# Second attention of a hybrid block: eight pairs of batches instead of four groups of four, and the causal mask of the row maxima added by VectorE head by head instead of by mask products on TensorE

## The reference, cut to what matters

```python
def _L2_attn_ref(x, wq, wk, wv, wo, ...):          # x: 16 batches, 256 tokens, 32 channels
    q = _rope(proj(wq, ...).reshape(B, S, 4, 8), cos, sin).transpose(0, 2, 1, 3)
    k = _rope(proj(wk, ...).reshape(B, S, 4, 8), cos, sin).transpose(0, 2, 1, 3)
    v = proj(wv, ...).reshape(B, S, 4, 8).transpose(0, 2, 1, 3)
    scores = jnp.einsum('bhqd,bhkd->bhqk', q, k) * 8 ** -0.5
    causal = jnp.triu(jnp.ones((S, S), dtype=bool), k=1)
    scores = jnp.where(causal[None, None], -jnp.inf, scores)
    attn = jax.nn.softmax(scores, axis=-1)
    out = jnp.einsum('bhqk,bhkd->bhqd', attn, v)
    return out.transpose(0, 2, 1, 3).reshape(B, S, 32) @ wo.T
```

## Time and profile before

| | |
|---|---|
| median of 3 runs | 640.49 us (640.01 to 640.94) |
| the profiled execution | 640.55 us, of which the span from the first to the last instruction is 638.7 us |
| busy over the whole span | TensorE 456.9 us (72%), VectorE 239.4 us (37%), ScalarE 273.0 us (43%) |
| the second attention's stretch 201.76 to 291.77 us of the span | from its first mask product to the first product of the next layer norm |

### The profile page before, as it was taken

The page is one execution under the profiler, slowest core; times in us unless marked ns, Lnnn a source line. Parts: engine busy times, 40 slices in busy tenths (PEclk is TensorE's granted clock), DMA queues, the critical chain, the costliest instruction groups (busy, mean ns, idle before and its releaser), DMA issues.

```text
span 638.7 us, 10438 instructions
## 1 busy us (share of the span) xinstructions
PE 456.9 (72%) x4078; PEld 221.0 (35%) x4082; DVE 239.4 (37%) x576; ACT 273.0 (43%) x822; POOL 21.7 (3%) x21
## 2 busy tenths in 40 slices
PE   5466666667888698876466666665677999799544
PEld 3222222223443344442233333333224553455211
DVE  1422222224644456632500000000086894587443
ACT  2333333334565255553333333333465554755411
POOL 1000000000002500000000000000030000000000
PEclk9655555556899899997655555555579998999966
DMA  5000000000000000000000000000041100000001
GB/s 209 0 2 1 0 1 2 1 0 2 1 2 1 1 1 2 2 2 0 1 1 0 1 1 1 1 0 1 0 90 38 42 9 1 2 2 2 2 9 35
DMA packets 8377, 7.43 MB, mean 12 GB/s; under 512 B 3202, under 2 KB 8066, under 8 KB 8196
## 3 DMA queue, kind: packets, MB, share of 16 engines
q1 hardware_dynamic: 8324, 6.70, 3.5%
HBM read 4.99 MB, written 0.52 MB: 9 GB/s over the span
## 4 chain that ended last, share of the span: by engine, by line
PE 64%; ACT 17%; DVE 9%; issue 7%; DMA 1%; SPq 1%; DVEq 1%; ACTq 0%
PE ps L410 18%; ACT arena L431 11%; PE ps L368 4%; PE ps L377 4%; PE ps L817 3%; PE ps L1122 3%; PE ps L1085 2%; PE ps L386 2%; PE ps L1101 2%; PE ps L811 2%; PE ps L326 2%; PE ps L1089 2%; DVE arena L1720 2%; PE ps L1143 1%; PE ps L1274 1%
## 5 line engine op out<-in xcount | busy, mean ns | idle before, releaser
L410 PE MATMUL ps<-arena,wsb 16*16 16x16 f32 (+1 forms) x1024 | 131.2, 206 | 103.8 <-ACT arena L431 102.9
L431 ACT ACTIVATE arena<-ps 16x16 f32<-16x16 f32 (+1 forms) x512 | 96.0, 188 | 183.5 <-PE ps L410 183.5
L410 PEld LDWEIGHTS ps<-arena,wsb 16*16 16x16 f32 (+1 forms) x1024 | 76.5, 118 | 192.4 <-ACT arena L431 184.5
L440 DVE TENSOR_TENSOR X<-X,ps 128x128 f32<-128x128 f32 x8 | 2.3, 288 | 137.4 <-PE ps L377 137.4
L1503 ACT ACTIVATE arena<-ps 128x512 f32<-128x512 f32 x72 | 40.8, 595 | 26.8 <-PE ps L1089 24.3
L1906 DVE TENSOR_TENSOR arena<-arena,ps 128x512 f32<-128x512 f32 x64 | 42.0, 682 | 17.3 <-ACT arena L1503 13.5
L1720 DVE TENSOR_REDUCE arena<-ps 128x4 f32<-128x512 f32 x48 | 30.6, 684 | 29.6 <-PE ps L817 29.6
L1374 ACT ACTIVATE arena<-ps 128x512 f32<-128x512 f32 x48 | 25.6, 593 | 25.4 <-PE ps L833 25.4
L817 PE MATMUL ps<-arena 32*128 32x512 f32 x96 | 25.5, 677 | 4.3 <-ACT arena L1374 3.3
L1085 PE MATMUL ps<-csb 128*128 128x512 bf16 x64 | 24.7, 385 | 2.7 <-DVE sq L464 1.8
L823 PE MATMUL ps<-arena 32*128 32x512 f32 x96 | 25.5, 679 | 1.2 <-ACT arena L1374 1.2
(11 more groups left out here) (300 smaller groups left out, 680.7 us busy)
## 6 DMA issues: line engine op xcount, KB each, us to landing
wsb<-weights SPq DMA_DIRECT2D x1, 2056.5 KB, 9.8
arena<-w SPq DMA_DIRECT2D x20, 64.0 KB
arena<-xn SPq DMA_DIRECT2D x9, 128.0 KB, 2.6
wsb<-weights SPq DMA_DIRECT2D x1, 549.5 KB, 4.4
X<-x SPq DMA_DIRECT2D x1, 512.0 KB, 3.6
out<-arena SPq DMA_DIRECT2D x2, 256.0 KB, 2.3
arena<-w_biases SPq DMA_DIRECT2D x20, 17.0 KB
csb<-consts SPq DMA_DIRECT2D x1, 130.0 KB, 9.7
```

The source lines that it names most:

```text
L410: nc.tensor.matmul(step_columns(k, rows, r), w_state, states[0:rows, :, :, t].rearrange("p g j -> p (g j)"), start=False, stop=True, skip_ ...
L431: nc.scalar.activation(states[0:rows, :, :, t + 1].rearrange("p g j -> p (g j)"), step_columns(t // STEP_BANK, rows, t % STEP_BANK), func) ...
```

## The change

The second attention goes by pairs of batches: `k` = 0 to 7, with batches 2 and 3 of group `k // 2` where `k` is even, and 0 and 1 where it is odd. S of pair `k + 1` runs with T of pair `k`, again in quads of one part, still with four different groups of rows. There are now seven passes of three mixed quads and a last one of T alone, in place of three passes of six and a last one of T alone for four batches. `max_copies2`, `max_rows2`, `maxima2` and `offsets2` run once a pair, so eight times and not four. `max_rows2` moves from ahead of a quad's masks to behind them.

S has no mask products any more; T keeps its own. Where a part is masked, VectorE takes the maxima by four instructions, one a head, each adding a bfloat16 mask from SBUF to 128 x 128 of the bank, writing the sum back and keeping the running maximum. Each of the four compiles to two instructions, a main one and one that writes the maximum (128 x 1) out. Part 1 keeps its one reduction.

Ahead of the first mixed quad only six units of S (pair 0) remain, the fourth projection and the projection of values stand together, and some copies of ScalarE and GpSimd change order. A `memset` of `max_copies` is new.

```diff
-        def unit_s2(j, part, g):
...
+        PAIRS = 2 * J
+
+        def pair2(k):
+            return k // 2, (0, 1) if k % 2 else (2, 3)
...
+        def unit_s2(k, part, i):
+            if k == 0:
+                return 2 * part + i
+            return 6 + 12 * (k - 1) + G * part + 2 * i
+
+        def unit_t2(k, part, i):
+            if k == PAIRS - 1:
+                return 6 + 12 * k + 2 * part + i
+            return 6 + 12 * k + G * part + 2 * i + 1
...
-                for g, turned in zip(s_batches, t_batches):
-                    masks2(part, [unit_s2(j + 1, part, g)], "mask_above")
-                    masks2(part, [unit_t2(j, part, turned)], "mask_below")
...
+            for k in range(PAIRS):
+                for part in range(3):
...
+                    for i in range(2):
+                        if k < PAIRS - 1:
+                            bank_free2(unit_s2(k + 1, part, i))
+                        mask2(part, unit_t2(k, part, i))
+                    if part == 0:
+                        max_rows2(k)
...
+                    for i in range(2):
+                        if k < PAIRS - 1:
+                            scores2(k + 1, part, i)
+                    for i in range(2):
+                        turned_scores2(k, part, i)
+                    offsets2(k, part)
...
+                    if part == 0 and k > 0:
+                        values2(k - 1, 2)
+                    if part > 0:
+                        values2(k, part - 1)
+                    if part == 0 and k in (3, 5, 7):
+                        out2((k - 3) // 2)
...
-            def max2_of(j, part, g):
-                dve.wait_ge(s["L2 scores"], count_s2(j, part, g) + 1)
-                nc.vector.reduce_max(max2[:, part, g, :], ps[:, bank2(unit_s2(j, part, g)), :].rearrange("p (h k) -> p h k", h=HEADS), AX)\
+            def max2_of(k, part, i):
+                dve.wait_ge(s["L2 scores"], count2(k, part, i) + 1)
+                if part != 1:
+                    for h in range(HEADS):
+                        ins = nc.vector.tensor_tensor_reduce(*[ps[:, bank2(unit_s2(k, part, i)), h * P:(h + 1) * P]] * 2, CB("mask_above"),
+                                                             1.0, MASKED, ALU.add, ALU.max,
+                                                             max2[:, part, pair2(k)[1][i], h:h + 1])
+                    ins.then_inc(s["L2 max"], 1)
+                    return
...
+            for k in range(PAIRS):
+                max_copies2(k)
+                offsets2(k)
+                for part in range(3):
+                    if k < PAIRS - 1:
+                        for i in range(2):
+                            max2_of(k + 1, part, i)
+                    if part == 0 and k > 0:
+                        denominators2(k - 1)
+                    if part == 1 and k in (3, 5, 7):
+                        added2((k - 3) // 2)
+                    if part == 2 and k > 0:
+                        attended2(k - 1)
```

More of the change, by code:

```diff
@@ L798, in _ @@
             project2(1, 1, 6, 7)
+            project2(0, 1, 1, 5)
             q2, k2 = (qk[:, i, :].rearrange("p (j t) -> p j t", j=J) for i in range(2))
             qh, kh = (by_head[:, i].rearrange("p h (j t) -> p h j t", j=J) for i in range(2))
[L802 to L823, removed]
+            def bank_free2(unit):
+                if unit >= RING2:
+                    drained, count = DRAINED2[unit - RING2]
+                    pe.wait_ge(s[drained], count)
+                if unit == 4:
+                    pe.wait_ge(s["L2 copied"], 4)
@@ new lines, in mask2, with scores2 @@
+            def mask2(part, unit):
+                bank_free2(unit)
+                if part != 1:
+                    nc.tensor.matmul(ps[:, bank2(unit), :], CB("identb"), CB("mask_below").unsqueeze(1).to_broadcast([P, HEADS, P]),
+                                     start=True, stop=False, skip_group_check=True)
+            def scores2(k, part, i):
+                j, batches = pair2(k)
+                (qt, kt), rows = PARTS2[part], slice(C * batches[i], C * (batches[i] + 1))
+                nc.tensor.matmul(ps[:, bank2(unit_s2(k, part, i)), :], q2[rows, j, qt * P:(qt + 1) * P], kh[rows, :, j, kt * P:(kt + 1) * P],
+                                 start=True, stop=True, skip_group_check=True).then_inc(s["L2 scores"], 1)
@@ L829, in offsets2 @@
                 qt = PARTS2[part][0]
                 for h in range(HEADS):
[L831 to L834, removed]
+                    for i, g in enumerate(pair2(k)[1]):
+                        rows, own = slice(C * g, C * (g + 1)), qt * HEADS + h
+                        mm = nc.tensor.matmul(ps[:, bank2(unit_t2(k, part, i)), h * P:(h + 1) * P],
+                                              CB("own_row")[rows, own:own + 1].to_broadcast([C, P]), offset2[rows, :],
@@ L933, in _ @@
-            values2(J - 1, 1, (0, 1))
-            values2(J - 1, 2, (2, 3))
-            out2(J - 2)
-            values2(J - 1, 2, (0, 1))
+                for i in range(2):
+                    bank_free2(unit_s2(0, part, i))
+                    scores2(0, part, i)
+            pe.wait_ge(s["L2 copied"], 4)
+            for jt in range(J * TT):
+                mm = nc.tensor.matmul(ps[:, 5 + jt // 4, (jt % 4) * P:(jt % 4 + 1) * P], xn[:, jt * P:(jt + 1) * P], wqkv[:, 2, :],
+                                      start=True, stop=True)
@@ L937, in _ @@
+            values2(PAIRS - 1, 2)
             out2(J - 1)
@@ L1366, in maxima2 @@
[L1366 to L1374 removed]
+            by_head_scalar(0, slice(0, T))
@@ L1375, in exp2, with inverse2 @@
+            def exp2(k, part, i):
+                act.wait_ge(s["L2 scores T"], count2(k, part, i) + 1)
+                if k >= 2 and part == 0:
+                    act.wait_ge(s["pv"], J + k - 1)
+                nc.scalar.activation(prob2[:, G * part + pair2(k)[1][i], :], ps[:, bank2(unit_t2(k, part, i)), :], ACT.Exp, scale=HD ** -0.5)\
                     .then_inc(s["L2 exp"], 1)
-            def inverse2(j, pair):
-                own = 2 * j + pair
-                cols = halves(den)[1 - pair]
-                act.wait_ge(s["den"], J + own + 1)
+            def inverse2(k):
+                cols = halves(den)[1 - k % 2]
+                act.wait_ge(s["den"], J + k + 1)
@@ L1408, in _ @@
+            inverse2(PAIRS - 1)
             norm_scalar(act, 2)
```

257 lines of the change are left out of this document (89 added, 168 removed).

## The result

| | before | changed |
|---|---|---|
| median of the runs, us | 640.72 (640.01 to 642.46, 4 runs) | 650.28 (649.64 to 650.77, 4 runs) |
| the profiled execution, us | 640.55, span 638.7 | 649.64, span 647.7 |
| ratio to before | | 1.0145, 95% interval 1.0122 to 1.0167 |
| first mixed scores start at | 217.75 | 209.88 |
| pair to pair (before: half a group of 18.74) | 9.37 | 10.73 |

The kernel is slower by 9.6 us between the medians. These rows of the changed kernel carry the last three lines of the table: the scores of the first and of the last pair, the last `max_rows2`, and the next norm.

What follows compares the result with a forecast made beforehand. The loop through VectorE's maxima was taken to bound the second attention. Loop loss 19.6 us less 7.6 at the beginning and 3.6 at the end gave 8.4 on 640.55: 649.0 us, range 640 to 670.

Steps and rivals of the forecast that it cites:

- first mixed scores: Beginning, ahead of the loop: six units in place of twelve, start at 210.26 against 217.82, saving 7.56 us.
- The loop: Second attention: scores, VectorE's maxima, bank free, next scores set the pace; 11.06 us a pair.
- 6.74 + 4D: Sum of the three scores-to-scores steps of one pair in the loop; 11.06 us with D = 1.08.
- D: VectorE's masked maximum for one unit: 4 x (0.20 + 0.07), 1.08 us, in place of one instruction of 0.60.
- The rival of the free second instruction: VectorE's masked maximum: writing out hides behind the next head's main one, D 0.80 to 0.85, 640 to 642; chance 0.12.
- no overlap: Rival, VectorE's masked maximum: nothing overlaps, D from 1.40 (659) to 1.72 (669); chance 0.20.
- The estimate of 0.32 a head: VectorE's masked maximum by the skill page: a head costs 0.26 + 0.06, D 1.28, time 655.
- seven pairs: The loop's whole length: 77.42 us against 57.85 before, 19.6 us lost.
- last scores to the next norm: End of the second attention: 12.5 us in place of 16.10, 3.6 us saved.
- later layers: Everything outside the stretch 201.76 to 291.77 us, taken as it is.
- My clock rival: TensorE's clock falls in the loop, busy share 58%: 3.5 us a pair, 24 in all, 673; chance 0.10.
- The removed masks: TensorE's mask products, 0.52 us of a masked quad, covered by the loop; predicted worth nothing.

Runs made afterwards that it cites:

- pairs_busy: Changed kernel plus unread products of 512 columns in TensorE's waits, five between part 0 and part 1, four between pairs; 644.58 us, ratio 1.0063.
- pairs_moved: Changed kernel with `attended2` of pair k - 2 moved behind the layout of the maxima of pair k; 641.72 us, ratio 1.004.
- groups_heads: Kernel before, still in groups of four, but S without mask products and with masked maxima by heads on VectorE; 649.53 us, ratio 1.0139.
- pairs_both: Changed kernel with the mask products of S added back on TensorE, so S is masked twice; 653.0 us, ratio 1.0197.
- pairs_heads: Against the pairs kernel with S's mask products and single reductions restored: masked units' reductions cut into four of 128 columns, no mask or accumulator; 644.87 us.
- pairs_moved_tail: Against pairs with mask products, single reductions and `attended2` moved: ten unread products in TensorE's wait ahead of the last `out2`; 632.02 us, ratio 0.9896.

## Why the prediction was right in its total, and where its sizes were not

**The loop: right.** Both timelines, the waits that changed sides, and four periods fit one formula, 6.74 + 4D: 9.13 measured at D = 0.60 (9.14), 9.90 at 0.80 (9.94), 10.73 and 10.70 at 1.00 (10.74). With `attended2` out of the way it is 0.42 less with heads and 0.47 less with products, where TensorE's own work comes to stand in two of three steps. The share of busy time (VectorE 37% before, 39% now) says nothing of it; the step at which an engine's work is waited for does.

**D: mis-sized.** I took 0.20 for the main instruction and 0.07 for writing the maximum out behind it, 1.08 for a unit. The rows show another split: the read-out starts together with the next main instruction, and main ones follow each other after 0.25, 1.00 for a unit. That the sum came near owes something to luck, for 0.20 was too low for this main instruction (a plain reduction of 128 columns has it, mask, write-back and accumulator add 0.05) and 0.07 too high. The rival of the free second instruction described the order of the two rightly, but its D of 0.80 to 0.85 is out, and no overlap (1.40 and more) is out as well. On that one the Trainium skill, "VectorE: DVE Perf Modes", section "Two Vector instructions with no wait between them", has an accumulator's operation as two instructions that are not held when their quarters match, and the trace agrees: 0.25 from head to head with a main record of 0.33. The estimate of 0.32 a head, from the section "The TRN2 errata" of the same page of the Trainium skill, is not borne out: the rows have 0.25.

**The sum, term by term** (us of the span, predicted and in the profile of the changed kernel):

| term | predicted | measured |
|---|---|---|
| first mixed scores | 210.26 | 209.88 |
| seven pairs | 77.42 | 76.74 (12.37 + 6 x 10.73) |
| last scores to the next norm | 12.5 | 17.24 |
| the norm starts at | 300.2 | 303.86 |
| from there to the end of the span | 346.9, as before | 343.8 |
| the span | 647.1 | 647.7 |

Two terms were off by more than a microsecond, and nearly cancelled. The **end** was predicted without the half clock, 12.5; in this trace it ran at 0.50 from 288 us on and took 4.7 longer. Otherwise it was right to 0.4: in *pairs_busy* the same stretch is 12.57 from `max_rows2`, whose scores follow 0.42 later. The **later layers** were "taken as they are" and were 3.1 us shorter.

The **seven pairs** look right to 0.7, but three misses cancel there as well. D was 0.08 too high, 28 times, 2.2 us. The first pair was given an `attended2` that it does not have; as in *pairs_moved* a pair without it takes 10.31 at full clock, 0.42 less. And the first pair took 12.37, so the half clock cost it about 2.1. That the total is right to about 1 us therefore owes something to luck, in the loop and around it.

**The clock.** My clock rival had the mechanism and put it into the wrong place, into every pair, for 24 us; it came in the first pair and behind the last scores. The busy share that it started from was too low: T has four mask products a pair, 1.04 us and not 0.52, and TensorE was busy for 38.82 of the 53 us from 222 to 275, 73% and not 58%.

**The removed masks: right for the loop.** From pair to pair they are worth nothing (10.70 against 10.73). Ahead of the loop they are worth something, which the prediction put at nothing: the first six units take 3.56 us without them and 6.40 with them. In the kernel before they were worth about 1 us a group (2.14 in place of 3.2); I had read that loop as bound by VectorE at each masked step, and at two of four it was not by VectorE alone.

**What the pairs brought.** With products they save 2.9 us. With maxima by heads they save nothing (650.28 against 649.53 for *groups_heads*). The layout, `attended2` and the turn of the maxima come once a pair on the chain that the heads have lengthened, 10.73 a pair against 20.88 for two. The half clock has its part in it too: in *pairs_busy*, without it, the next norm starts at 297.58, and in *groups_heads* at 300.25.

**Open:** why the clock fell at the end of the changed kernel and not in *pairs_moved*, whose TensorE has the same instructions in the same order; and why the time behind the norm differs. The wait ahead of the last `max_rows2` alone does not tell: it is 1.33 us in the changed kernel, 0.91 in *pairs_moved*, and 1.33 again in *pairs_both*, where the clock was 1.00 from 288 to 297.

## What to carry to other kernels

Before work is taken from a full engine and given to one that is busy for 37%, read who is waited for at that step: the second engine's time may be a whole term of the loop, and the first one's may be cover. Splitting an operation can cost time by itself: here half of the loss (0.77 of 1.60 us a pair) came from four short reductions in place of one, before any mask was added. And look what short work stands between the last operation of such a chain and its consumer: moving one multiplication behind the layout gave 0.42 us a pair, and the same move with products made TensorE the bound in most of the pair.

## What the runs showed of the hardware that was not expected

- An accumulator's read-out (0.14 us in the records) starts together with the next main instruction, so it adds no step of its own to the 0.25 from head to head. Where the layout comes next, it starts 0.18 behind the start of the last read-out (232.48 to 232.66).
- With ten products that nobody reads in a wait of 2.90 us, the granted clock stayed at 1.00 over what follows (0.57 without them from 284 to 288 us), and two groups of products took about half the time.
- The layers behind the second attention, with the same instructions, took 346.9 us of the span before, 343.8 in the changed kernel, 346.1 in *pairs_busy*, 348.0 in *pairs_both*, 345.4 in *pairs_heads*, 343.7 in *pairs_moved* and 340.3 in *pairs_moved_tail*, where the norm's products alone are 1.8 us shorter. Part of it is the clock there. A stretch of 30 us from about the same scan on, first in the kernel before, then in the changed one, had 0.89 and 1.00:

```profile
470.00:500.00 30.00, 24.73 (x217) 11.98 (x217) 23.95 (x54) 15.05 (x26) 0.00 (x0) 0.89 0.18 41
```

```profile
482.00:512.00 30.00, 25.32 (x260) 13.18 (x261) 26.67 (x59) 16.50 (x29) 0.00 (x0) 1.00 0.18 40
```

- In the executions of one and the same kernel, the time and the mean granted clock go together. Of the 24 of the kernel before that belong to *pairs_moved*, the four with a mean granted clock of 0.730 took 641.5 to 642.1 us, two with 0.741 took 636.9 and 637.2, and the one with 0.744 took 634.6. Of the ten of *pairs_moved*, eight with 0.739 to 0.742 took 640.8 to 642.6, and the two with 0.734 and 0.736 took 645.6 and 644.4. The four of the changed kernel had 0.728 to 0.732.

So 3 us and more of a profile's total can come from a place that an edit never touched, and a change of that size is to be judged by the stretch it touches, and by many runs.
